# A straight scatter list, an early product of the input, and logits pair by pair in one two-layer kernel

## The reference

```python
# layer 0, on xn = layernorm(x)
adj = zeros(N, N).at[src, dst].set(1.0)                  # 33792 edges
a   = (q @ k.T) / sqrt(512);  a = a*adj + (1-adj)*NEG
x   = x + softmax(a) @ v + linear_attention(xn)          # the second has no softmax
x   = x + one_of_16_experts(layernorm(x))
# layer 1
x   = x + graph_mlp(xn, segment_mean(edge_attr)) + splat_attention(xn)
x   = x + mlp_with_64_way_router(layernorm(x))

def splat_weights(tok):                                   # 8 heads, 16 splats each
    d2 = sum(tok**2) + c_sq - 2 * tok @ centers.T
    return exp(-d2 * inv_var) * amps
qw, kw = splat_weights(q), splat_weights(k)
logits = qw @ kw.T / temperature                          # per head, 1024 x 1024
out    = softmax(logits) @ v  ->  @ out_w.T
```

## Time and profile before

| | us |
|---|---|
| median of three runs (1316.8 to 1320.16) | 1317.12 |
| the profiled execution | 1318.35 |
| its span, first to last instruction | 1316.5 |
| PE, DVE, POOL, ACT busy | 882.7, 531.5, 421.3, 342.9 |
| mean granted TensorE clock, share of full speed | 0.829 |

### The profile page before, as it was taken

The page is one execution under the profiler, slowest core; times in us unless marked ns, Lnnn a source line. Parts: engine busy times, 40 slices in busy tenths (PEclk is TensorE's granted clock), DMA queues, the critical chain, the costliest instruction groups (busy, mean ns, idle before and its releaser), DMA issues.

```text
span 1316.5 us, 11299 instructions
## 1 busy us (share of the span) xinstructions
PE 882.7 (67%) x3882; PEld 602.4 (46%) x3882; DVE 531.5 (40%) x855; ACT 342.9 (26%) x514; POOL 421.3 (32%) x407
## 2 busy tenths in 40 slices
PE   4902000131019899999991993899998678898978
PEld 2502000120017688887870432677765434444565
DVE  5400000110012367406654118632245678764377
ACT  1200000100000244223220112121332057788521
POOL 5777777776630000000003105400000035456401
PEclk9955555565557899999996995999999879998999
DMA  9501000310000000300123974010100000000001
GB/s 342 201 0 32 0 0 0 120 41 0 0 0 0 1 0 0 128 0 33 61 100 105 309 272 128 27 64 0 64 0 1 33 1 0 2 2 1 1 5 64
DMA packets 45599, 70.51 MB, mean 54 GB/s; under 512 B 12577, under 2 KB 13729, under 8 KB 45554
## 3 DMA queue, kind: packets, MB, share of 16 engines
q1 hardware_dynamic: 33266, 60.39, 13.8%
q0 software_dynamic: 10752, 6.90, 2.0%
q10 hardware_dynamic: 1536, 2.62, 0.6%
HBM read 58.22 MB, written 11.67 MB: 53 GB/s over the span
## 4 chain that ended last, share of the span: by engine, by line
PE 55%; another core or an unknown queue 24%; DVE 12%; ACT 3%; issue 3%; DMA 2%; POOL 1%; SPq 0%; ACTq 0%; DVEq 0%; PEldq 0%; POOLq 0%
PE bank L782 11%; PE bank L784 10%; PE bank L783 10%; PE bank L930 6%; PE bank L998 4%; PE bank L838 2%; DVE key L1848 2%; PE bank L1081 1%; PE bank L1112 1%; PE bank L886 1%; ACT slot L1192 1%; DVE cols L1451 1%; DVE xT L1445 1%; PE bank L1053 1%
## 5 line engine op out<-in xcount | busy, mean ns | idle before, releaser
L720 POOL DMA_INDIRECT not_adjacent<-zero,keyring x264 | 263.8, 999 | 99.5 <-issue 85.6
L782 PE MATMUL bank<-slot 128*128 128x512 f32 (+1 forms) x212 | 88.1, 415 | 187.4 <-issue 156.6
L762 POOL TENSOR_TENSOR slot<-arena,slot 128x512 fp32r<-128x512 f32 x43 | 66.6, 1549 | 274.3 <-ACT slot L1366 274.0
L782 PEld LDWEIGHTS bank<-slot 128*128 128x128 f32 x212 | 43.5, 205 | 198.4 <-issue 166.3
L1445 DVE TENSOR_TENSOR slot<-bank,slot 128x512 fp32r<-128x512 f32 x44 | 29.2, 687 | 249.4 <-issue 151.9
L1198 ACT ACTIVATE slot<-bank 128x512 fp32r<-128x512 f32 x60 | 35.0, 597 | 363.4 <-remote 184.0
L735 POOL DMA_INDIRECT expert_rows<-xn,idx x8 | 8.3, 1037 | 329.2 <-DVE idx L1712 327.1
L782 PE MATMUL bank<-xT,slot 128*128 128x512 f32 (+1 forms) x248 | 105.0, 423 | 7.7 <-DVE xT L1445 5.8
L783 PE MATMUL bank<-slot 128*128 128x512 f32 (+1 forms) x212 | 85.5, 403 | 21.7 <-issue 21.7
L784 PE MATMUL bank<-slot 128*128 128x512 f32 (+1 forms) x212 | 85.3, 402 | 20.2 <-issue 20.2
L783 PE MATMUL bank<-xT,slot 128*128 128x512 f32 (+1 forms) x248 | 97.7, 394 | 0.0
(11 more groups left out here) (276 smaller groups left out, 1651.4 us busy)
## 6 DMA issues: line engine op xcount, KB each, us to landing
arena<-in_ewT SPq DMA_DIRECT2D x16, 1024.0 KB, 8.8
arena<-in_edge_attr SPq DMA_DIRECT2D x3, 2816.0 KB, 24.1
not_adjacent<-zero,keyring POOLq DMA_INDIRECT x264
wraw<-in_qkvT SPq DMA_DIRECT2D x3, 1024.0 KB
expert_rows<-rowb SPq DMA_DIRECT2D x1, 2560.0 KB
wraw<-in_L_ffn_expert_b POOLq DMA_DIRECT2D x16, 160.0 KB, 5.8
expert_results<-wraw ACTq DMA_DIRECT2D x16, 160.0 KB, 5.8
not_adjacent<-agg SPq DMA_DIRECT2D x1, 2048.0 KB, 8.4
```

The source lines that it names most:

```text
L720: pool.indirect_dma_start(adjd, bass.IndirectOffsetOnAxis(ap=keyring[:, h, b:b + 1], axis=0), zero16[:, :], None).then_inc(scattered[h], 16)
L762: pool.tensor_tensor(psplit(n % 3, 1, 1), pexp[:, n % 3, 1, :], f32(psplit(n % 3, 0, 1)), ALU.subtract).then_inc(p_lo[1], 1)
L782: pe.matmul(out, L[1], R[0], start=start, stop=False, **kw)
```

## The change

Three edits in one kernel.

1. *Scatter list.* `keyring`, its copies and the loop go. 264 indirect DMAs are written out and read their column of `key` directly; the wait for the batch of the same parity stays.
2. *Early product.* `XB(t)`, 12 matmuls of the input with B, becomes a product of its own after V, added to `xres` by DVE. `AV` keeps the 24 matmuls. `mask(0)`, `mask(1)`, `scale(0)` and the first exponential follow behind V and XB.
3. *Pair by pair.* `splat_steps` interleaves, for each pair c, both sides' p and d2 with the 16 logits of pair c - 1; the last pair's stand between the V1 products. Logits have two pairs of banks. `vector_order` puts DVE's weights two logits behind. The amplitudes of both sides go into q's weights, so that k's aren't scaled. The attention loop keeps E and O; ACT copies head 1 alone, DVE head 0 (`p_high`), which there waits for the O of three units before. Lv is split on ACT and DVE after the last p of side k; F is loaded after all maxima.

```diff
+            for q in range(SCATTERS // BATCH):
+                if q >= 2:
+                    pool.wait_ge(scattered[q % 2], q // 2 * (16 * BATCH))
+                for j in range(q * BATCH, (q + 1) * BATCH):
+                    pool.indirect_dma_start(adjd, bass.IndirectOffsetOnAxis(ap=key[:, j:j + 1], axis=0),
+                                            zero16[:, :], None).then_inc(scattered[q % 2], 16)
...
+            for t in range(T):
+                product(("XB", t), lambda k: xt(t, k), lambda k: sl(1, k))
+            for t in range(T):
+                emptied(pe, "V", t)
+            for t in range(T - 4, T):
+                emptied(pe, "XB", t)
...
                 o = open_bank("AV", t)
-                for k in range(C):
-                    mm3(o, xt(t, k), sl(1, k), k == 0, False)
...
+def splat_steps():
+    steps = []
+    for c in range(PAIRS + 1):
+        logits = [("L", c - 1, it, jh) for it in range(T) for jh in range(2)] if c else []
+        if c < PAIRS:
+            work = [("p", side, c, th) for side in "qk" for th in range(2)]
+            work += [("d2", side, c, th) for side in "qk" for th in range(2)]
+            behind = [0, 2, 3, 3, 2, 2, 2, 2]
+        else:
+            work = [("V1", t) for t in range(T)]
+            behind = [2] * T
+        for i, (job, count) in enumerate(zip(work, behind)):
+            steps.append(job)
+            steps += logits[:count]
+            logits = logits[count:]
+            if i == 1 and c > 1:
+                steps.append(("mT", c - 2))
+    return steps
...
             dve.wait_ge(bias_added, 1)
+            for t in range(T):
+                finished(dve, "XB", t)
+                dve.tensor_tensor(xres[:, t, :], at("XB", t), xres[:, t, :], ALU.add).then_inc(evicted[bank_of[("XB", t)]], 1)
+            mask(0)
+            mask(1)
+            scale(0)
...
+            def p_high(n):
+                emptied(dve, "E", n)
+                if n >= 3:
+                    used(dve, n - 3)
+                dve.tensor_copy(psplit(n % 3, 0, 0), pexp[:, n % 3, 0, :]).then_inc(p_hi[0], 1)
```

More of the change, by code:

```diff
@@ L159, in plan_jobs @@
     add("csq")
[L160 to L165, removed]
+    for step in splat_steps():
+        if step[0] == "p":
+            add(*step, bank=4 + step[3])
+        elif step[0] == "d2":
+            add(*step, bank=6 + step[3])
+        elif step[0] == "L":
+            add(*step, bank=2 * step[3])
+        elif step[0] == "V1":
+            add(*step, bank=4 + step[1] % 4)
+        else:
+            add(*step, bank=0)
     for step in attention_steps():
@@ L169, in plan_jobs @@
             add(*step, bank=0)
-        elif step[0] == "L":
-            add(*step, bank=6 if step[1] == 0 and step[3] else 0)
-        elif step[0] in ("V1", "X3"):
+        elif step[0] == "X3":
             add(*step, bank=2 + step[1] % 4)
@@ L204, in last_of_group, with vector_order @@
     return n % T == T - 1
+def splat_steps():
[6 more added lines that the diff above has]
+            behind = [0, 2, 3, 3, 2, 2, 2, 2]
+        else:
+            work = [("V1", t) for t in range(T)]
[7 more added lines that the diff above has]
+    return steps
+def vector_order():
+    order, held = [], []
+    for step in splat_steps():
+        if step[0] == "d2":
+            held.append([step, 2])
+            continue
+        if step[0] in ("p", "V1", "mT"):
+            if step[0] != "mT" and step[-1] == 0:
+                order += [h[0] for h in held]
+                held = []
+            order.append(step)
+            continue
+        order.append(step)
+        for h in held:
+            h[1] -= 1
+        order += [h[0] for h in held if h[1] <= 0]
+        held = [h for h in held if h[1] > 0]
+    assert not held
+    return order
 def attention_steps():
     steps = []
[L210 to L218, removed]
+    lag = 3
     for n in range(UNITS + lag):
@@ L1061, in krows, with logits @@
                 return slice(64 * b, 64 * b + n)
-            pe.wait_ge(st_ready, 4 * PAIRS)
-            pe.wait_ge(w_split, windex["Lv"] + 1)
-            for side in "qk":
-                for c in range(PAIRS):
-                    for th in range(2):
-                        emptied(pe, "d2", side, c, th)
+            def logits(step):
+                _, c, it, jh = step
+                if (it, jh) == (0, 0):
+                    pe.wait_ge(st_ready, 4 * (c + 1))
+                    if c == 0:
+                        emptied(pe, "csq")
+                        for t in range(TH):
+                            emptied(pe, "HW", 1, 1, t)
+                open_bank(*step)
+                for b in range(2):
+                    r = krows(b, KROWS)
+                    ins = pe.matmul(bank[:, bank_of[step] + b, :], stack(2, c, r, it * P, (it + 1) * P),
+                                    stack(3, c, r, jh * HALF, (jh + 1) * HALF), start=True, stop=True)
+                close(ins)
@@ L1270, in _ @@
                 hi(("V", t))
[L1271 to L1272 removed]
+            exponentials(0)
             for t in range(T):
```

268 lines of the change are left out of this document (124 added, 144 removed).

## The result

The change made the kernel slower by 0.7%: 1327.48 us (median of five runs, 1324.63 to 1330.21) against 1316.8 (five runs, 1316.52 to 1320.16), a ratio of 1.0072 with a 95% interval of 1.0055 to 1.009. The forecast was 1300 and faster, its range 1280 to 1326.

What follows compares the result with a forecast made beforehand. It took PE's slow stage, released by the scatter's end, as the early bound, with PE, DVE and ACT sharing later stages. -19 + 15 + 14 - 27 = -17 took 1318.35 to 1301, median 1300, range 1280 to 1326.

Steps and rivals of the forecast that it cites:

- The scatter list, -19: Scatter stage: writing the list straight, without copies, ends PE's slow stage earlier; -19 us, bounds -11 and -21.
- What PE gets: Scatter stage: PE gains 23.6 less 4.5, since some 18 matmuls left at the scatter's end take 9 us against 4.8.
- POOL's part: Scatter issue on POOL: removed copies, their waits and three long gaps end the scatter 23.6 us earlier, bounds 16 and 24.
- The lag of 4.8: Time from the last scatter to the last slow product, 378.88 to 383.67; read as the scatter's end releasing the stage.
- Rival (a): Scatter stage: PE's slow stage isn't released by the scatter, so the list brings nothing, 1319 us; chance 0.20.
- Rival (b): Scatter stage: PE's slowness hangs on POOL's loop or copies and goes with them; some 1090 us; chance 0.06.
- The early product, +15: First attention: XB +21.8, later first transposes +5.1, shorter loop -11.6; together +15 us, bounds +10 and +27.
- The start-up, +26.9: Before the first attention's transposes: XB's products +21.8 and masks and scale waiting behind its evictions +5.1 us.
- The splat stage, +14: Splat weights, interleaved logits and V1: 146 us with the split of Lv, against 132; +14, bounds -6 and +25.
- rival (c): New splat stage: PE's granted clock falls while it waits for maxima; at 1.2 GHz throughout, 1376 us; chance 0.09.
- The second attention, -27: Second attention without logits and maxima: eight groups 139.6 plus split of Lo 4.2, 144 against 171; bounds -17 and -31.
- the dear bound of 2.4 a unit: Second attention: if DVE's copy holds up POOL's subtraction wholly, 2.4 us a unit, 154 us for the stage.

Runs made afterwards that it cites:

- e8: Changed kernel with 120 of its 264 scatters and masks 0 and 1 and scale 0 ahead of the XB additions: 1140.34 us, one run.
- e11: Changed kernel with 192 of its 264 scatters: 1242.85 us, one run.
- e12: Changed kernel with 24 more scatters, which write the same flags again: 1361.66 us, one run.
- e13: Changed kernel with 144 scatters, each issued only when the one before has landed: 1118.49 us, one run.
- e15: Changed kernel, all 264 scatters, waiting for landing after every second one: 1259.53 us, ratio 0.9682 to the kernel before.
- e17: Changed kernel, all 264 scatters, waiting for landing after every fourth one: 1173.88 us, ratio 0.8903 to the kernel before.
- e5: The changed kernel again, unaltered, on a quiet occasion: 1065.75 us, ratio 0.9634 to the kernel before.
- e2: Kernel before with the early product alone, on a quiet occasion: 1094.14 us, ratio 0.9871.
- e18: Changed kernel, waiting for landing after every fourth scatter, without waits from batch 17 on; quiet occasion: 1151.63 us, ratio 1.0397 to the kernel before.
- e14: Changed kernel, all 264 scatters, a tiny POOL write ahead of each: 1278.5 us, ratio 0.9782 to the kernel before.
- e16: Changed kernel, all 264 scatters, waiting for landing after every third one: 1197.57 us, ratio 0.908 to the kernel before.

## Why the prediction was wrong

**The scatter list, -19, measured 0 where the forecast was tested.** The step that failed is "What PE gets: ... some 18 left at 0.4 to 0.6 are 9 us against 4.8". POOL's part was right (-22.2 at the end, of -23.6). The reading that the scatter's end releases the stage was right too (e8, e11, e12). Wrong was that PE's pace under the scatter would stay as it was, and that it would be quick 5 us behind the end. With the loop's pauses gone, GK's 12 matmuls take 33.6 instead of 12 to 25, so that at the scatter's end none of B's four products has come out where two had at the same moment before (309.40, 344.39), and the slow pace lasts past it until the split stands 28 behind instead of 5. That slower scatters free PE is shown by e13 and e15 to e17; that it was the loop's pauses which made GK quicker is argued from one pair of traces, and VK was as slow with them (129 against 134). The lag of 4.8 had been read as PE finishing its last matmuls, though PE's rows have all of B started by 323.38: it was a backlog, of work or of signals, which the prediction didn't look for. That POOL's 22 gained and the longer lag cancel to 0.4 is chance. Rival (a) named the outcome for the list, 0, with a chance of 0.20, but not this mechanism. (Its own sum is a little off too: 9 less 4.8 is 4.2 and not 4.5, which changes nothing.)

The Trainium skill (SBUF — State Buffer, Who interferes with whom) has DMA never contending with a compute engine and PE never waiting on anyone. By it, as the prediction used it, the list brought 0. The measurement bears out the 0 but not the reason, since the scatter does bear on PE's stage: 192 scatters instead of 264 took 85 us off (e11, one run). The section is about SBUF's ports, and no run here tells whether these are the way.

**Rival (b), 0.06, was half a truth.** Where PE isn't slow, the first mask waits for the scatter and the changed kernel takes 1066, 24 below the 1090 that it gave. But neither loop nor copies decide: the straight list had the slow stage, and with the loop PE was quick on a quiet occasion.

**The early product, +15, measured +19.2.** The start-up, +26.9, came out at +26.8. The loop gives 7.6 instead of 11.6. PE's timeline:

```profile
634.09 1.94 PE L989 MATMUL bank<-kst,arena 128*128 128x128 f32 x8 [7.19 <-DVE arena L1653]
...
643.94 1.04 PE L989 MATMUL bank<-kst,arena 128*128 128x128 f32 x8
...
651.75 1.09 PE L989 MATMUL bank<-kst,arena 128*128 128x128 f32 x8
...
659.67 1.09 PE L989 MATMUL bank<-kst,arena 128*128 128x128 f32 x8
```

The first iteration takes 9.85: behind the wait of 7.19 PE runs at 1.2 GHz (granted 0.50 from 634 to 636), and the eight transposes last 1.94 instead of 1.04. The others take 7.7 to 8.0, also the last three for which I had 7.4.

**The splat stage, +14, measured +21.** It took 149.9 instead of 146, and 3 more come from the other side: the stage of before was taken as 132 from its window and lasts 129.0 from its first eviction. The first pair took 17.8 as worked out, the next two 29.9 and 31.1 instead of 30. The term that was too small is the last pair with the split of Lv. DVE's and PE's timelines:

```profile
1036.48 3.49 DVE L1868 TENSOR_REDUCE key<-bank 128x2 f32<-128x1024 f32 x3 [1.99 <-PE bank L1085]
1044.17 2.29 DVE L1467 TENSOR_TENSOR slot<-wraw,slot 128x2048 fp32r<-128x2048 f32 x1 [4.21 <-ACT slot L1236]
1046.38 3.48 DVE L1868 TENSOR_REDUCE key<-bank 128x2 f32<-128x1024 f32 x3
```

```profile
1047.66 0.79 PE L1085 MATMUL bank<-slot 48*128 48x512 f32 x2 [5.76 <-DVE key L1868]
1048.38 2.07 PE L1108 MATMUL bank<-xn,kst 128*128 128x512 f32 x2
...
1053.24 1.13 PE L1108 MATMUL bank<-xn,kst 128*128 128x512 f32 x2
```

DVE's queue stands 4.21 for ACT's half of the split and 2.29 for its own, 6.5 instead of 5; the maxima behind it come late, PE waits 5.76, and its clock falls (granted 0.50 from 1048.0 to 1052.4): two matmuls of d2 take 2.07, then 1.13 again. The pair takes 38.2 instead of 35. That is rival (c) for some 5 us, not for the stage.

**The second attention, -27, measured -33.3, and +3.5 behind it.** ACT's timeline, from the first to the last exponential, with the evictions of two finished groups:

```profile
1099.69 1.94 ACT L1411 ACTIVATE arena<-bank 128x1024 f32<-128x1024 f32 x2 [3.64 <-PE bank L1149]
...
1137.34 1.07 ACT L1422 ACTIVATE arena<-bank 65x512 f32<-65x512 f32 x2
...
1154.30 1.06 ACT L1422 ACTIVATE arena<-bank 65x512 f32<-65x512 f32 x2
...
1235.86 1.03 ACT L1411 ACTIVATE arena<-bank 128x1024 f32<-128x1024 f32 x1 [0.42 <-PE bank L1149]
```

A group takes 16.96 instead of the 17.45 of the earlier trace rows, 3.9 over the stage. POOL's subtraction takes 1.40 on average of the 64, against 1.55 before, so the dear bound of 2.4 a unit was far off. The rest is in the ends of the stretch: 63 distances and not 64 units lie between the first and the last exponential, and the first ones follow each other faster. The split of Lo costs about the 4 that it was given. Of the gain 1.8 return behind the last exponential (7.2 from its start to the next eviction, at 1243.05, against 5.4): the last O products wait 0.49 and 1.52 for DVE's subtractions, where 0.23 for POOL's was the only wait. And 1.9 more follow from one wait of PE:

```profile
1274.01 2.64 PE L814 MATMUL bank<-kst,xn 128*128 128x128 f32 x16 [3.29 <-DVE arena L1928]
...
1282.74 1.91 PE L814 MATMUL bank<-kst,xn 128*128 128x128 f32 x16
```

The same 16 transposes take 2.64 instead of 1.91, and eight of the matmuls behind them 0.43 apart instead of 0.23. In the trace of before this wait was 1.68 long and the clock stayed at full speed.

Together the stages other than the list's were forecast at +2 and measured at +9.5; the list missed by 19.

## What to carry to other kernels

Ask of every pause that an edit removes who works in it. With a pause of 1.1 us more in four scatters the changed kernel was 11% faster than before where PE suffered from their density; with 0.7 less in twelve it got nothing from the earlier end. Read both ends of a wait, too: when a reader waits 20 us for a product, look at when the writer's matmuls start in its own rows. When an engine's end falls together with another's, the lag between the two is a measurement of that one arrangement and doesn't move with it. And a bound that comes and goes from one occasion to the next must be met both ways before an edit is judged: straight list with pairs and without the early product was faster on both (1308.49 against 1317.93, 1079.06 against 1106.16), the whole change only on quiet ones, and the list in fours has been shown only on a slow one.

## What the runs showed of the hardware

On a slow occasion products come at 2.8 us for each matmul with its weight load under a dense scatter, whatever its size: 12 of 512 columns take 33.6, the 48 of VK with 128 columns 134. So it is a price per matmul with its load and not per column. It isn't TensorE's clock: at a granted clock of 0.50 the matmuls of 347.5 to 353 start 0.43 apart. PE's rows run ahead of this pace by up to some 30 matmuls. VK's first 24 start 0.21 apart (179.31 to 184.28), and only then do they stand apart by 1.4, 2.8 or 3.5, multiples of 0.70; B's first 36 start by 358.34, when not one of its products is out. PE's timeline of e11 as its slow stage ends, 14 to 20 us behind the last scatter (over at 258.55):

```profile
272.70 0.27 PE L807 MATMUL bank<-slot 128*128 128x128 f32 x1 [2.53 <-issue]
275.50 0.27 PE L808 MATMUL bank<-slot 128*128 128x128 f32 x1 [2.53 <-issue]
276.90 0.27 PE L806 MATMUL bank<-slot 128*128 128x128 f32 x1 [1.14 <-issue]
279.00 0.26 PE L807 MATMUL bank<-slot 128*128 128x128 f32 x1 [1.83 <-issue]
```

One thing in the traces goes with it. A scatter raises its semaphore 16 times, and the trace records it. Counted over the two semaphores of the scatter:

```
quiet:              e5 4216 of 4224   e2 4217 of 4224   e18 4221 of 4224
slow:               before 655, changed 593, e14 682 of 4224, e12 613 of 4608, e11 381 of 3072, e8 344 of 1920
slow, looser list:  e13 2304 of 2304, e15 3953, e16 3462, e17 3155 of 4224
```

Where PE was slow, some six records of seven are missing; on quiet occasions nearly none are. In between the share grows with the density, 6% in e15, 18% in e16 and 25% in e17, as PE's delay from WkT to V does (0.5, 12 and 20 us against e18). And it hangs on PE too: in e17 about half are missing from 180 to 260, while PE is at its small matmuls, and none from 360 on, while PE only waits. It isn't a measure of PE's pace, though: e14 lacks as many as the changed kernel, with PE about twice as fast. The Trainium skill (NOTIFIC — the notification-queue block, Overflow: three behaviours, one of which stalls the engine) says that a full queue of such records can drop them or hold up the engine that makes them. The missing records, a price per matmul, products signalled long after their matmuls start, and a slow pace that outlasts the scatter would fit a queue that drains more slowly on some occasions; no run here shows the holding up itself, and another cause with these signs isn't excluded, since no run varied the recording. Every execution here, the timed ones too, was recorded, so no run tells whether PE is slow when nothing is recorded. If the recording is the cause, the slow stage is a cost of measuring and a kernel should be judged by the quiet occasions, where the change gained 3.7%. That stays open, and so does what differs between the occasions: all executions made together were of one kind, with the kernel before at 1105 to 1110 on three occasions and at 1294 to 1322 on five.
